# Expert tile biases by TensorE products with a 0/1 table, and the low row halves of batches 2 and 3 by VectorE

## The reference, cut to what matters

```python
x = x + _L0_xattn_ref(ctx_1024, _layernorm(x))       # dynamic time warping; ends at 118 us here
xf = _layernorm(x).reshape(-1, 128)                  # 2048 tokens
scores = sigmoid(xf @ gate_w + bias)
top_scores, top_idx = top_k(scores, 2)
up   = einsum('th,ehi->tei', xf, up_w) + up_b        # 8 experts, 128 -> 512
hact = gelu(up)
eo   = einsum('tei,eih->teh', hact, down_w) + down_b
combined = einsum('teh,te->th', eo * 0.1, w)         # w: normalised top scores, else 0
shared = (gelu(xf @ sw_up + sb_up) @ sw_down + sb_down) * 0.1
out = shared + combined
out = out / (max(abs(out)) + 1e-6);  x = x + out
```

## Time and profile before

| what | value |
|---|---|
| runs, one execution each | 290.87, 291.84, 289.36 us (median 290.87) |
| profiled execution: span from first to last instruction | 264.9 us |
| profiled execution: its own device time | not listed; its span is 26.0 us under the median of the runs |
| busy share of the span: PE, DVE, ACT, POOL | 65%, 75%, 53%, 42% |
| first scatter of batches 1 to 3 | at 142.66 us |
| first up-product of the expert loop | at 174.72 us |
| last down-products of the expert loop end, tail begins | at about 242.9 us |

### The profile page before, as it was taken

The page is one execution under the profiler, slowest core; times in us unless marked ns, Lnnn a source line. Parts: engine busy times, 40 slices in busy tenths (PEclk is TensorE's granted clock), DMA queues, the critical chain, the costliest instruction groups (busy, mean ns, idle before and its releaser), DMA issues.

```text
span 264.9 us, 5441 instructions
## 1 busy us (share of the span) xinstructions
PE 171.1 (65%) x1351; PEld 113.8 (43%) x1352; DVE 198.2 (75%) x941; ACT 139.9 (53%) x336; POOL 110.2 (42%) x169
## 2 busy tenths in 40 slices
PE   1492029999000001465645978979999999998991
PEld 0240014443000000363322323359999999997640
DVE  2853899999994492588779799779888888883045
ACT  5552027993000402308997666567888788874031
POOL 8400040000000001462277878874777777777200
PEclk9998558999755555555557899999999999999999
DMA  6002969530403000000112144343433322000355
GB/s 195 26 1 95 117 210 333 175 52 4 84 1 66 28 0 0 4 2 0 45 56 70 45 146 144 100 133 93 126 95 95 105 84 83 28 16 2 109 208 158
DMA packets 34562, 22.08 MB, mean 83 GB/s; under 512 B 15251, under 2 KB 30577, under 8 KB 34533
## 3 DMA queue, kind: packets, MB, share of 16 engines
q1 hardware_dynamic: 31062, 16.18, 23.9%
q0 software_dynamic: 2496, 4.24, 4.9%
q10 hardware_dynamic: 975, 1.33, 1.5%
HBM read 12.57 MB, written 9.03 MB: 82 GB/s over the span
## 4 chain that ended last, share of the span: by engine, by line
PE 37%; DVE 33%; POOL 8%; ACT 6%; DMA 6%; issue 6%; DVEq 1%; SPq 1%; ACTq 0%; POOLq 0%
PE bank L1052 8%; PE bank L1053 7%; DVE arena_b L1225 7%; PE bank L1054 7%; POOL sorted_dram L700 7%; DVE edge L1216 4%; DVE arena_f L1220 3%; DVE arena_c L1217 3%; PE bank L1162 3%; ACT x_sb L825 2%; DVE arena_f L1227 2%; PE bank L1105 2%; PE bank L949 2%; PE bank L985 1%; POOL row_and_place L708 1%
## 5 line engine op out<-in xcount | busy, mean ns | idle before, releaser
L735 POOL DMA_INDIRECT expert_dram<-arena_d,arena_f x46 | 49.4, 1074 | 18.5 <-issue 15.7
L897 ACT ACTIVATE arena_f<-bank,tile_bias 128x256 f32<-128x256 f32 x92 | 35.9, 474 | 1.3 <-PE bank L1054 0.6
L1052 PE MATMUL bank<-arena_a,up_hi 128*128 128x256 f16 (+1 forms) x108 | 32.7, 302 | 4.6 <-ACT x L814 2.2
L1052 PE MATMUL bank<-down_hi,arena_d 128*128 x184 | 32.5, 219 | 1.3 <-DVE arena_g L1525 1.3
L1525 DVE TENSOR_TENSOR arena_g<-arena_f,arena_d 128x512 f16<-128x512 f32 x46 | 32.0, 695 | 1.6
L1053 PE MATMUL bank<-arena_a,up_hi 128*128 128x256 f16 (+1 forms) x108 | 32.4, 300 | 0.0
L1054 PE MATMUL bank<-arena_a,up_lo 128*128 128x256 f16 (+1 forms) x108 | 32.4, 300 | 0.0
L1054 PE MATMUL bank<-down_hi,arena_g 128*128 x184 | 32.3, 219 | 0.0
L1053 PE MATMUL bank<-down_lo,arena_d 128*128 x184 | 32.3, 219 | 0.0
L673 POOL COPY met_at<-arena_b 32x3 f16 (+1 forms) x26 | 3.9, 181 | 66.6 <-DVE arena_b L1285 62.4
L985 PE MATMUL bank<-arena_b,minus_one 128*128 (+1 forms) x26 | 3.9, 184 | 42.6 <-issue 42.6
(11 more groups left out here) (258 smaller groups left out, 466.9 us busy)
## 6 DMA issues: line engine op xcount, KB each, us to landing
arena_f<-sorted_dram SPq DMA_DIRECT2D x23, 130.0 KB, 2.2
arena_d<-in_L_ffn_up_w SPq DMA_DIRECT2D x6, 256.0 KB, 5.7
arena_d<-in_L_ffn_down_w SPq DMA_DIRECT2D x5, 256.0 KB, 5.7
sorted_dram<-padding SPq DMA_DIRECT2D x9, 130.0 KB
x_sb<-in_x SPq DMA_DIRECT2D x4, 256.0 KB, 4.4
arena_c<-row_and_place SPq DMA_DIRECT2D x4, 256.0 KB, 2.8
arena_b<-expert_dram SPq DMA_DIRECT2D x4, 256.0 KB, 4.6
arena_c<-expert_dram ACTq DMA_DIRECT2D x4, 256.0 KB, 5.0
```

The costliest lines, as they stand in the source:

```text
L735: pool.indirect_dma_start(out=expert_dram.ap(), in_=y_row[:, j % Y_SLOTS, n, :], in_offset=None, out_offset=bass.IndirectOffsetOnAxis(ap=p ...
L897: last = act.activation(hid[:, k, m, cols], banks[UP_BANK + HALVES * k + m][:, cols], ACT.Gelu, bias=bias, scale=1.0 / WSCALE)
L1052: pe.matmul(o, a_hi, b_hi, start=start, stop=False)
```

## The change

It does two things. First, the bias of each tile. VectorE no longer compares and sums on all partitions. It compares `turn_of` with the partition's own tile number on 23 partitions (`own_tiles`) and sums for each expert, so that `of_expert` is now a 0/1 table [23 tiles, 8 experts]. TensorE turns it (`turn_table`, behind the first shared down-product), ScalarE copies it out as `tiles_of` [8, 23], TensorE multiplies it in four products with the biases as they lie in DRAM, one row per expert (`spread_biases`, behind the second shared down-product), and ScalarE copies the result out as `tile_bias`, whose two inner dimensions have changed places. Both land in bank 5. Second, the low halves of batches 2 and 3 are made by VectorE, one instruction of 512 columns per batch; the copies by SyncE and the scatters of these batches wait for it by a semaphore of their own. Names of semaphores that changed without effect are left out.

```diff
+LOW_BY_POOL = 2
...
-        bias_ld = sb("bias_ld", [(E + 1) * NCH, P])
-        up_bias = sb("up_bias", [P, E + 1, NCH])
-        tile_bias = sb("tile_bias", [P, EXPERT_TILES, NCH])
+        bias_ld = sb("bias_ld", [NCH, P])
+        up_bias = sb("up_bias", [P, NCH])
+        bias_rows = sb("bias_rows", [E, I])
+        tile_bias = sb("tile_bias", [P, NCH, EXPERT_TILES])
...
+        own_tiles = sb("own_tiles", [P, E * TILES_EACH])
...
-        of_expert = sb("of_expert", [P, EXPERT_TILES, E])
-        biased = sb("biased", [P, EXPERT_TILES, E])
+        of_expert = sb("of_expert", [EXPERT_TILES, E])
+        tiles_of = sb("tiles_of", [E, EXPERT_TILES])
...
-            sp.dma_start(bias_ld[0:E * NCH, :], up_b.rearrange("e (c p) -> (e c) p", p=P)).then_inc(small_ld, 16)
-            sp.dma_start(bias_ld[E * NCH:(E + 1) * NCH, :], sb_up.rearrange("(c p) -> c p", p=P)
-                         ).then_inc(small_ld, 16)
+            sp.dma_start(bias_rows[:], up_b).then_inc(small_ld, 16)
+            sp.dma_start(bias_ld[:], sb_up.rearrange("(c p) -> c p", p=P)).then_inc(small_ld, 16)
             sp.dma_start(gate_ld[:], gate_w).then_inc(small_ld, 16)
...
-                sp.wait_ge(row_lo_by_pool, 1 + HALVES * b)
+                if b < LOW_BY_POOL:
+                    sp.wait_ge(row_lo_by_pool, 1 + HALVES * b)
+                else:
+                    sp.wait_ge(row_lo_by_dve, b - LOW_BY_POOL + 1)
                 sp.dma_start(row_and_place2[:, batch_tiles(b), 0:H], row_and_place[:, batch_tiles(b), 0:H]
                              ).then_inc(second_in[b], 16)
...
-            sp.wait_ge(table_ready, 2)
+            sp.wait_ge(table_ready, 3)
...
                     if k and t % TPB == 0:
                         pool.wait_ge(second_in[t // TPB], 16)
-                    elif t >= TPB and t % PARTS == 0:
+                    elif TPB <= t < LOW_BY_POOL * TPB and t % PARTS == 0:
                         pool.wait_ge(row_lo_by_pool, (t - TPB) // PARTS + 2)
+                    elif t >= LOW_BY_POOL * TPB and t % TPB == 0:
+                        pool.wait_ge(row_lo_by_dve, t // TPB - LOW_BY_POOL + 1)
                     src = row_and_place2 if k else row_and_place
                     pool.indirect_dma_start(
                         out=sorted_dram.ap(), in_=src[:, t, :], in_offset=None,
@@ -715,16 +721,9 @@
             scatter(1, PARTS, TPB, early_scattered)
             low_rows(TPB + PARTS)
             pool.wait_ge(slots_ready, TOP + 1)
-            scatter(0, TPB, 2 * TPB, early_scattered)
-            low_rows(2 * TPB)
-            scatter(0, 2 * TPB, 2 * TPB + PARTS, early_scattered)
-            low_rows(2 * TPB + PARTS)
-            scatter(0, 2 * TPB + PARTS, 3 * TPB, early_scattered)
+            scatter(0, TPB, EARLY_BATCHES * TPB, early_scattered)
             pool.wait_ge(slots_ready, TOP + 2)
-            scatter(1, TPB, TPB + PARTS, early_scattered)
-            low_rows(3 * TPB)
-            scatter(1, TPB + PARTS, 3 * TPB, early_scattered)
-            low_rows(3 * TPB + PARTS)
+            scatter(1, TPB, EARLY_BATCHES * TPB, early_scattered)
             for k in range(TOP):
                 scatter(k, EARLY_BATCHES * TPB, TILES, late_scattered)
...
+                    if n == 3 * NCH - 1:
+                        act.wait_ge(table_in_psum, 1)
+                        act.activation(tiles_of[:], banks[TABLE_BANK][0:E, 0:EXPERT_TILES], ACT.Copy
+                                       ).then_inc(table_by_act, 1)
+                act.wait_ge(table_in_psum, 2)
+                act.activation(tile_bias[:].rearrange("p c j -> p (c j)"),
+                               banks[TABLE_BANK][:, BIAS_COLUMN:BIAS_COLUMN + NCH * EXPERT_TILES], ACT.Copy
+                               ).then_inc(table_by_act, 1)
...
-                        bias = tile_bias[:, j:j + 1, m * (NCH // HALVES) + q]
+                        bias = tile_bias[:, m * (NCH // HALVES) + q, j:j + 1]
...
+            def turn_table():
+                pe.wait_ge(table_ready, 2)
+                pe.transpose(banks[TABLE_BANK][0:E, 0:EXPERT_TILES], of_expert[:],
+                             ident[0:EXPERT_TILES, 0:EXPERT_TILES]).then_inc(table_in_psum, 1)
+
+            def spread_biases():
+                pe.wait_ge(table_by_act, 1)
+                for c in range(NCH):
+                    first = BIAS_COLUMN + c * EXPERT_TILES
+                    mm = pe.matmul(banks[TABLE_BANK][:, first:first + EXPERT_TILES], bias_rows[:, c * P:(c + 1) * P],
+                                   tiles_of[:], start=True, stop=True)
+                mm.then_inc(table_in_psum, 1)
+
             def shared():
                 for b in range(B + 2):
                     if b < B:
@@ -1093,6 +1111,10 @@
                                      ).then_inc(gatesT_in_psum, 1)
                     if b >= 2:
                         shared_down(b - 2)
+                    if b == 2:
+                        turn_table()
+                    if b == 3:
+                        spread_biases()
...
-            def every_tile(v):
-                return v.unsqueeze(1).to_broadcast([P, EXPERT_TILES, E])
-
             def all_of(v):
                 return v[:].rearrange("p e i -> p (e i)")
+
+            def low_rows(g):
+                t = batch_tiles(g)
+                dve.wait_ge(row_hi_ready, g + 1)
+                dve.tensor_tensor(row_lo[:, t], y2[:, t, :], row_hi[:, t], ALU.subtract).then_inc(row_lo_by_dve, 1)
 
             dve.wait_ge(slots_ready, TOP * len(ROUTED))
             shared_half(0)
             shared_half(1)
+            low_rows(2)
             for k in range(TOP):
                 routed(dve.scalar_tensor_tensor(part[:, k], pick[:, k], WSCALE, per_tile(weight[k]),
                                                 ALU.mult, ALU.mult))
             dve.tensor_tensor(gates[:], part[:, 0], part[:, 1], ALU.add).then_inc(gates_ready, 1)
             shared_half(2)
+            low_rows(3)
...
+            dve.tensor_scalar(own_tiles[rows], all_of(turn_of)[rows], own_turn[rows, 0:1], None, ALU.is_equal)
...
             with nc.allow_low_precision(reason="one whole number and zeros"):
                 dve.tensor_reduce(tile_column[:], found2[rows], AX_X, ALU.add).then_inc(table_ready, 1)
+                dve.tensor_reduce(of_expert[:], own_tiles[rows].rearrange("p (e i) -> p e i", i=TILES_EACH), AX_X, ALU.add
+                                  ).then_inc(table_ready, 1)
                 routed(dve.tensor_reduce(tile_row_f[:], found[rows], AX_X, ALU.add))
             dve.tensor_scalar(tile_row[:], tile_row_f[:], float(PAD_ROW), None, ALU.add).then_inc(table_ready, 1)
             shared_half(7)
             shared_half(8)
-            turns = at_turn.rearrange("p (j i) -> p j i", i=TILES_EACH)
-            for e in range(E):
-                routed(dve.tensor_tensor(turns, turn_of[:, e].unsqueeze(1).to_broadcast([P, EXPERT_TILES, TILES_EACH]),
-                                         tile_no[:].unsqueeze(2).to_broadcast([P, EXPERT_TILES, TILES_EACH]), ALU.is_equal))
-                routed(dve.tensor_reduce(of_expert[:, :, e], turns, AX_X, ALU.add))
-                if e % 2 and e < E - 1:
-                    shared_half(9 + e // 2)
-            shared_half(12)
-            dve.wait_ge(up_bias_ready, 1)
-            for c in range(NCH):
-                routed(dve.tensor_tensor(biased[:], of_expert[:], every_tile(up_bias[:, 0:E, c]), ALU.mult))
-                ins = dve.tensor_reduce(tile_bias[:, :, c], biased[:], AX_X, ALU.add)
-                ins.then_inc(tile_bias_ready, 1)
-                dve.wait_ge(tile_bias_ready, c + 1)
-                if c < NCH - 1:
-                    shared_half(13 + c)
+            for n in range(9, B * NCH):
+                shared_half(n)
 
             def keep_turned(j, k):
                 dve.wait_ge(xT_in_psum, j + 1)
```

31 lines of the change are left out of this document (14 added, 17 removed).

## The result

The changed kernel took 298.22 us (median of 4 runs, 297.03 to 298.46) beside 291.36 for the kernel before in the same set of runs (4 runs, 289.36 to 292.34): ratio 1.023 [1.018, 1.028], **6.9 us slower**. Predicted were 288.0 us and a gain of 2.9. The profiled execution was 297.03 us long with a span of 295.3. Only 1.7 us lie around the span, not the 26.0 that the prediction laid there. Ratios here are of undisturbed runs alone and are not the quotients of the medians beside them; by the medians a gain can come out up to 0.7 us smaller.

The account below looks back on a forecast made before the run. The loop's start was taken as the bound, set by the later of the load's path (up-products at 171.8) and TensorE's (171.4), from 174.7. That gained 2.9: 290.87 - 2.9 = 288.0 us, own range 287.0 to 289.0, 8 in 10 286.0 to 290.0.

Parts of the forecast that it names:

- the 26.0: Around the profiled span: the execution was said to add 26.0 us to it, measured against the median.
- The sum: Whole kernel: the later path sets the loop's start, gaining 2.9 us; span 264.9 to 262.0, time 288.0 us.
- the loop and tail stay as long: From the loop's first up-product to the span's end: unchanged by the change, 90.2 us.
- the filler is 4 us of steady work: TensorE's 18 filler products before the last shared down-product: 4.0 us in all, beginning near 163.6.
- rival C: TensorE's clock returns later after the gates' pause: mild form 289.3 us, chance 0.1; slower kernel, 298, chance 0.05.
- Load's path: Early scatters to landing of the first loads: 2.9 us gained, up-products at 171.8.
- Scatter stretch: GpSimd's 16 scatters, lengthened when begun during VectorE's two-input reads: 0.3 us worse, bounds 2.3 better to 2.3 worse.
- Rival B: GpSimd's scatters no longer stretched: load's path gains 5.5 us, TensorE's path decides, 3.3 gained, 287.6 us; chance 0.1.
- a scatter of over 1.5: Sign on GpSimd's scatters that the prediction is wrong: one lasting over 1.5 us.
- TensorE's path: Shared products before the loop: last down-product begins 2.6 us earlier, at 167.6; up-products can start at 171.4.
- The sum of the two, 2.9: Loop start from both paths: load's path 171.8, TensorE's 171.4; the later decides, 2.9 us gained.
- Rival C, mild form: TensorE's low clock after the gates' pause lasts 3.4 us more, costing 1.7; gain 1.6, 289.3 us; chance 0.1.

Follow-up runs that it names:

- 291 chip: Chip, or chip state, of the result's runs: kernel before 291.36 us, changed kernel 298.22; its only trace is of the changed kernel.
- 267 chips: Four different chips in four more sets of runs: kernel before about 267 us, changed kernel 264 to 265.
- set 1: Kernel before and changed kernel rerun without edits, with each part alone: before 266.97 us, changed 264.65, ratio 0.989.
- third set: Against kernel before at 267.13 us: changed kernel 264.77; changed kernel with loads held back 271.82, without filler 265.09; low rows alone, first subtraction behind gates, 264.19.
- Fourth set: Changed kernel and each part alone against kernel before at 266.98 us: both parts 263.82, biases alone 267.18, low rows alone 264.63.
- first set: The result's own runs, changed kernel against kernel before: 298.22 us beside 291.36, ratio 1.023; not the later set 1.

## Why the prediction was wrong

**The step that failed is the last one of "The sum": "The execution adds 26.0 around its span, measured against the median".** Runs that list both have 1.6 to 3.3 us around the span, 1.7 in most. So about 24 of the 26.0 must have been inside the span, as time that the shown trace did not have; no trace of the kernel before shows it, and the changed kernel's shows gaps and a thinner loop. A trace whose span falls 9% below the median of its runs is not a trace of those runs; I turned that discrepancy into a constant instead of a rival. From it follow the next two faults: that the loop and tail stay as long (90.2 us forecast from the loop's start, 110.4 measured), and that the filler is 4 us of steady work (14.4 measured). The constant also put at nothing what the change does to that time: it was 24.4 us for the kernel before and 33.5 for the changed one, and these 9.1 outweigh the gain of 2.9. The text ahead of the prediction calls the 26.0 start and end of the execution; no run shows that. No rival held the outcome. The 298 that rival C names as its worst came by another way: the clock was full from 147.9 to 168.4, and fell after the gaps had begun. That its number was met is luck.

By its steps:

- *Load's path, 2.9 gained.* On the 291 chip the last early scatter ended at 164.26 (forecast 165.0) and the first load was issued at 167.72, 3.5 behind and not 2.2 (its register instructions began at 167.0). On the 267 chips the scatters ended 2.6 to 2.8 earlier counted from the first (forecast 2.4), and the first load followed 2.1 behind in all three sets. Right.
- *Scatter stretch 0.3 worse.* Busy 17.4 to 17.6 for the 16, against 17.6 before: nothing, within the bounds. Rival B's end of the stretch did not come: the scatter that begins during VectorE's subtractions is still stretched (1.46 to 1.47 for the first one in every trace). The sign "a scatter of over 1.5" did come: 2.11 on the 291 chip, 2.12 and 2.05 in sets 1 and 3. The sum of the sixteen stayed all the same, so it was no sign of a longer stretch.
- *TensorE's path, 2.6 at the last down-product.* Fourth set: 25.3 behind the first scatter instead of 27.5, 2.2 gained. The products were under-priced: 1.07 and 0.18, 1.3 in place of 0.6. ScalarE's two copies cost nothing, as said. The missed credit was VectorE's stalls under GpSimd, 2.6 us in its list.
- *The sum of the two, 2.9.* Counted from the first scatter to the first up-product, 2.7 to 2.9 in sets 3 and 4, 1.5 to 1.7 in set 1, by which trace of the kernel before is taken. As medians 2.3, 2.4 and 3.2 (sets 1, 3, 4). So the 2.9 was a fair size for the 267 chips, but by luck in part: TensorE's path was last and not the load's, its products cost more than priced and a credit was missed.
- *Rival C, mild form.* It happened in the profiled run of set 1 (6.8 us at 1.2 GHz where the earlier trace rows have 3.4), and the up-products came 1.2 later than in the other two sets. Its price was of the size given, 1.7. The same 6.8 stand in two variants of the third set.
- *What the parts were worth.* The prediction took the bias instructions as the main relief of TensorE's path. Alone they start the filler 1.0 earlier and bring nothing in time; the low rows alone bring all.

**What stays open.** Why one chip's sequencers stumble, and why the change makes them stumble more: 291.4 - 267.0 = 24.4 us for the kernel before, 298.2 - 264.7 = 33.5 for the changed one, 9.1 more. No instruction-fetch transfer lies in the trace from 154 to 187 us, so a visible fetch is not it. It is tempting to blame the loads, since in the kernel before the filler ended (169.7) before the first load was issued (170.16) and now runs under them. The trace speaks against that: the gaps begin at 162.75, before the loads, seven loads at their usual pace go with no gap, and gaps go on after the last load. Another rival was not tested: the same trace has lost a quarter of its semaphore events, from 130 us on and so before the gaps, and whether what lost them also held TensorE and SyncE up, or both have a third cause, one trace cannot tell. The runs meant to test the gaps (held-back loads, no filler, each part alone) all fell on chips without them, and there is no trace of the kernel before with them. Which part of the change brings the slower time on the 291 chip is therefore not known either.

No variant clearly beats the changed kernel where there are no gaps: without the filler 0.987 and 0.992, low rows alone 0.988 and 0.990, the low rows alone with the gates first 0.987, all within each other's intervals.

## What to carry to other kernels

Before you read a trace for its stages, hold its span against the runs that you will be measured by. If they differ by more than a few us, treat "the runs have something that this trace lacks" as a rival with a chance and ask which of your steps it would undo. When you price work on VectorE from a mean, look whether GpSimd's vector instructions lie under the long ones: moving those off GpSimd can shorten both lists. And where two paths end within 1 us of each other, as here, removing work from one of them alone can be worth nothing, as the biases alone were. Last, before a gap is called the engine's own, look whether the trace has all its semaphore events: without them a wait and a gap read alike.

## What the runs showed of the hardware

- The same kernel took 264.7 us on one chip and 298.2 in the first set (span against time 1.7 us apart in both), with the same granted clock over the whole execution (0.814 at spans of 264.4 and of 295.3). Where no wait stands in the code, the difference was time between instructions, on TensorE in multiples of 0.7 us, on SyncE in register instructions of up to 695 ns in place of 42. GpSimd's scatters kept their 0.30 us between them.
- GpSimd's vector work and VectorE's hold each other up: on VectorE 1.13 us for 0.35 (a comparison), 0.90 for 0.42 (a cast of 512 columns) and 0.69 for 0.22; on GpSimd a mean of 1052 ns for 904 with the denser list. A scatter's issue is held as well: 0.96 us mostly, about 1.47 where it begins just behind the start of a VectorE subtraction of 512 columns, and 2.1 where two such follow each other (in set 1's changed kernel both begin at 154.54 and the subtractions take 1.27). The Trainium skill, "SBUF — State Buffer", section "Who interferes with whom", has the shared port as an exclusive lock. The rows above agree on the two compute engines; on its inference that a tensor_tensor leaves a DMA's issue alone, the 1.47 speaks against it in every trace here.
